# Two attention layers with experts on one core: the first layer's normals move to GpSimd, and twelve of eighteen weight products move from the first layer's end to the second layer's start

## What is computed

```
x = x + xattn0(layernorm(x), ctx)            # 16 heads of 16
x = x + experts(layernorm(x))                # 8 experts, one per token, 512 places each, else x
x = x + xattn1(layernorm(x), ctx)            # 16 heads, biases, then relu(.@W1+b1)@W2+b2
x = x + cell(layernorm(x))                   # 6 nodes of attention, 8 heads of 32, then a layernorm
# one node c of the cell; src, edge: fixed small tables
q = ew[c,0]*(nodes[src_q] @ We[eq] + be[eq]) ; k, v likewise with ew[c,1], ew[c,2]
nodes[c] = act_w[c]*mha(q,k,v; Wq[c],Wk[c],Wv[c],Wo[c]) + q
```

## Time and profile before

| | us |
|---|---|
| median of 3 runs | 4257.91 (4254.85 to 4258.33) |
| the profiled execution | 4261.87 |
| its span, first to last instruction | 4260.1 |
| PE busy | 4052.2 (95%) |
| ACT busy | 2647.2 (62%) |
| DVE busy | 2515.5 (59%) |
| POOL busy | 1774.9 (42%) |
| mean granted clock of PE, share of 2.4 GHz | 0.978 |

### The profile page before, as it was taken

The page is one execution under the profiler, slowest core; times in us unless marked ns, Lnnn a source line. Parts: engine busy times, 40 slices in busy tenths (PEclk is TensorE's granted clock), DMA queues, the critical chain, the costliest instruction groups (busy, mean ns, idle before and its releaser), DMA issues.

```text
span 4260.1 us, 100693 instructions
## 1 busy us (share of the span) xinstructions
PE 4052.2 (95%) x38276; PEld 3431.3 (81%) x38276; DVE 2515.5 (59%) x6280; ACT 2647.2 (62%) x11818; POOL 1774.9 (42%) x1883
## 2 busy tenths in 40 slices
...
DMA packets 117867, 129.75 MB, mean 30 GB/s; under 512 B 12006, under 2 KB 110676, under 8 KB 117264
## 3 DMA queue, kind: packets, MB, share of 16 engines
...
## 4 chain that ended last, share of the span: by engine, by line
PE 58%; DVE 9%; ACT 5%; POOL 3%; issue 1%; DMA 0%; SPq 0%; POOLq 0%; DVEq 0%
PE c_product L1297 26%; PE c_product L1308 12%; PE c_product L1348 8%; PE c_scores L1338 6%; ACT c_front_probs L1118 4%; PE c_product L1371 4%; DVE c_neg_max L1173 2%; DVE c_xn L1158 2%; DVE c_routed L1158 1%; PE c_product L1359 1%; DVE c_x L1183 1%; POOL c_rstd L1064 1%; ACT c_probs L1118 1%; POOL c_probs L1076 1%; PE c_product L1285 1%
## 5 line engine op out<-in xcount | busy, mean ns | idle before, releaser
L1118 ACT ACTIVATE c_probs<-c_scores,c_neg_max 128x128 f32<-128x128 f32 x3072 | 1081.9, 407 | 480.5 <-DVE c_neg_max L1173 480.5
L1076 POOL TENSOR_TENSOR c_probs<-c_probs,c_row_inv 128x512 f32<-128x512 f32 x768 | 790.5, 1041 | 1211.3 <-DVE c_row_inv L1176 1208.7
L1297 PE MATMUL c_product<-c_nodes,cell_w 128*128 128x256 f32 x4352 | 1056.9, 383 | 2.7 <-DVE c_nodes L1164 1.0
L1297 PEld LDWEIGHTS c_product<-c_nodes,cell_w 128*128 128x128 f32 x4352 | 803.5, 190 | 124.8 <-issue 19.6
L1173 DVE TENSOR_REDUCE c_neg_max<-c_scores 128x4 f32<-128x512 f32 x1024 | 635.7, 683 | 254.9 <-PE c_scores L1338 254.9
L1118 ACT ACTIVATION_READ_ACCUMULATOR c_probs<-c_scores,c_neg_max 128x1 f32 x3072 | 757.7, 247 | 0.0
L1124 ACT COPY c_probsT<-c_product 128x512 f32<-128x512 f32 x768 | 413.3, 613 | 440.4 <-PE c_product L1348 440.4
L1308 PE MATMUL c_product<-cell_w,c_nodes 128*128 128x256 f32 x1792 | 435.4, 383 | 0.0
L1118 ACT ACTIVATE c_front_probs<-c_scores,c_neg_max 128x128 f32<-128x128 f32 x1024 | 358.3, 403 | 116.7 <-DVE c_neg_max L1173 116.7
L1348 PE MATMUL c_product<-consts_sb,c_probs 128*128 128x128 f32 x3072 | 398.8, 276 | 14.8 <-POOL c_probs L1076 13.7
L1348 PEld LDWEIGHTS c_product<-consts_sb,c_probs 128*128 128x128 f32 x3072 | 350.9, 142 | 47.8 <-POOL c_probs L1076 19.8
...
## 6 DMA issues: line engine op xcount, KB each, us to landing
...
a_x<-in_x SPq DMA_DIRECT2D x32, 256.0 KB, 3.4
a_ctxT<-in_ctx_pairsT SPq DMA_DIRECT2D x32, 256.0 KB, 3.5
x<-a_x SPq DMA_DIRECT2D x32, 256.0 KB, 2.1
xn<-a_xn SPq DMA_DIRECT2D x32, 256.0 KB, 2.2
c_routed<-xn SPq DMA_DIRECT2D x32, 256.0 KB, 2.9
c_x<-x SPq DMA_DIRECT2D x32, 256.0 KB, 3.0
c_ctxT<-in_ctx_pairsT SPq DMA_DIRECT2D x32, 256.0 KB, 2.7
```

The costliest lines, as they stand in the source:

```text
L1076: nc.gpsimd.tensor_tensor(e, e, rinv[:, i, r].unsqueeze(2).broadcast_to([P, 4, T]), ALU.mult).then_inc(norm_made, 1)
L1118: a = nc.scalar.activation(probs(n)[:, r, k], S[r][:, k], ACT.Exp, bias=nmax[:, i, r, k:k + 1], accum_out=rsum[:, i, r, k:k + 1])
L1297: i = T_.matmul(m[:, u], w[:, k, u * P:(u + 1) * P], src[:, k], start=n == 0, stop=n == last)
```

## The change

1. First layer: `nm` and `nm1` (four instructions a job, 128x256 with two operations each) go from DVE to POOL, with buffers of statistics doubled; DVE's `bn_aggr` gets a wait for the normal two jobs back. `K^O` goes from ACT to DVE, behind `K^`. `w.s` is taken out. `xn1` has 6 places instead of 8. All four order tables are new, with longer lags (`r.n:4` becomes `r.n:6`).
2. F0 to F5 and B0 to B5 stay at the first layer's end, the other twelve pairs go to the second layer's first steps. Their inputs go through a ring of four that lies in the buffers of the cell's probabilities, unused until then. Loads of number 6 to 9 are started by ACT, those from 10 on by SP.
3. Experts: SP loads the plain weights for node e-1 behind the loads of expert e, POOL scales them. DVE turns the first rows out (`rows_turned(0)`) before it waits for `b2`, not after.
4. Second layer: the rows, the context and three weights are loaded first, by SP; the other weights by ACT, each with a semaphore of its own. Before, SP started all twelve ahead of the rows. The four order tables are new.

The core of the diff (of the tables, the lines that the prediction speaks of):

```diff
 FIRST_POOL_ORDER = """
-S0.n1:1 S0.n2:1 S0.n3:1 S1.n0:1 S1.n1:1 S1.n2:1 w.s:6 rs1:2 S1.n3:1 put:9 rs:-1 S0.n0:0
+rs:1 nm:1 rs1:4 S0.n0:2 nm1:4 S0.n1:2 S1.n0:2 S1.n1:2 S1.n3:2 S1.n2:2 S0.n3:2 S0.n2:2 put:9
 """
 FUSE_PE_PLACES = """
-...
-r.n:0 F8 F9 B8 B9 F10 F11 B10 B11 F12 F13 B12 B13 F14 F15 B14 B15 F16 F17 B16 B17
+Tn:1 F0
+L:1 B0
+Tn:0 F1
+L:0 B1 F2 F3
+r.n:0 B2 B3 F4 F5 B4 B5
 """
+            def normal(src, dst, i, j, made):
+                pool.wait_ge(rstd_made[i], j + 1)
+                for b in range(PAIR):
+                    k = nc.gpsimd.tensor_scalar(dst[:, b], src[:, b], mv[:, i, j % 2, b, 0:1], rstd[:, i, j % 2, b:b + 1],
+                                                ALU.subtract, ALU.mult)
+                k.then_inc(made, 1)
...
+                elif n == "nm":
+                    if j >= 1:
+                        pool.wait_ge(prod, n_prod["Tx", j - 1])
+                    normal(xt[:, j % X_RING], xn, 0, j, xn_made)
...
+                    V.tensor_scalar(kE[:, o], m, cst[:, C_EVEN:C_EVEN + 1], None, ALU.mult)
+                    V.tensor_scalar(kO[:, o], m, cst[:, C_ODD:C_ODD + 1], None, ALU.mult).then_inc(prod_used, 1)
...
+            rows_turned(0)
             dve.wait_ge(b2_in, 16)
-            rows_turned(0)
...
 PE_ORDER = """
-V1:1 K2:1 Q4:2 T1.0:1 f.Tb0.1:0 S4:2 T1.1:1 K5:2 V4:2 A1:1 f.Ab0:0 O1:1 T4.0:2 T4.1:2 f.Sb1:0 A4:2 Q2:1 O4:2
+f.Tb0.1:0 V1:1 O3:2 K2:1 T1.0:1 Q4:2 T1.1:1 S4:2 f.V:0 K5:2 V4:2 A1:1 T4.0:2 f.Sb1:0 O1:1 f.Ab0:0 T4.1:2 Q2:1
+f.Tb1.0:0 A4:2 S2:1 f.Tb1.1:0 O4:2 f.Ab1:0 Q5:2 f.W1a:0 f.W1b:0 T2.0:1 S5:2 f.W2:0 K3:1 V2:1 T2.1:1 V5:2
+LATE_FUSE_PE_PLACES = """
+start:0 F6 B6 F7 B7 F8 B8 F9 B9 F10
+f.Tx:0 B10
+f.Q:0 F11
+f.Sb0:0 B11 F12 F13 B12 B13 F14
+f.Tb0.0:0 B14
+f.Ab0:0 F15 F16 B15
+f.Tb1.0:0 B16 F17
+f.Tb1.1:0 B17
+"""
...
+            load_rows(0)
+            load_context(0)
+            for t, a, got in ((wk, "L1_xattn_Wk_rows", wk_in), (wq, "L1_xattn_Wq", wq_in), (wv, "L1_xattn_Wv_rows", wv_in)):
+                sp.dma_start(t[:], halves(io[a])).then_inc(got, 16)
+            fuse_load(FUSED_FIRST + LATE_RING)
+            load_rows(1)
+            for n in range(FUSED_FIRST + LATE_RING + 1, len(fused)):
+                fuse_load(n)
+            load_context(1)
```

More of the change, by code:

```diff
@@ L64, in cell_plan, with fused_weights @@
     return plan
+def fused_weights(plan):
+    return [(c, k, plan[c]["edge"][k]) for c in range(NODES) for k in (TO_Q, TO_K, TO_V)]
 def unfold(table, jobs):
@@ L71, in unfold, with with_fused @@
     return [(name, k - s) for k in range(min(first, 0), jobs + last) for name, s in order if 0 <= k - s < jobs]
+def with_fused(order, table, job_of, at):
+    order = list(order)
+    for line in table.strip().splitlines():
+        behind, *pieces = line.split()
+        name, k = behind.split(":")
+        i = 0 if name == "start" else order.index((name, job_of(int(k)))) + 1
+        order[i:i] = [(p, at) for p in pieces]
+    return order
 def counted(order, test):
@@ L138, in phase_first_layer @@
     W2 = PAIR * T
[L139 removed]
+    X_RING, ROW_RING, GROUP = 4, 6, 4
     MASK_JOBS, SENDS, RING = 4, 3, 3
     plan = cell_plan()
[L142 removed]
+    fused = fused_weights(plan)
     SCALE = 1.0 / np.sqrt(D // CELL_HEADS)
[L144 removed]
     PAIRS_OF_HEADS = D // 32
@@ L868 @@
 PE_ORDER = """
-f.Tx:0 T0.1:1 S3:2 f.K:0 f.Q:0 K4:2 K1:1 A0:1 f.Sb0:0 T3.0:2 O0:1 f.V:0 T3.1:2 Q1:1 f.Tb0.0:0 A3:2 S1:1 O3:2
-V1:1 K2:1 Q4:2 T1.0:1 f.Tb0.1:0 S4:2 T1.1:1 K5:2 V4:2 A1:1 f.Ab0:0 O1:1 T4.0:2 T4.1:2 f.Sb1:0 A4:2 Q2:1 O4:2
-f.Tb1.0:0 f.Tb1.1:0 S2:1 V5:2 f.Ab1:0 Q5:2 f.W1a:0 f.W1b:0 S5:2 f.W2:0 K3:1 T2.0:1 V2:1 f.Txn:0 T5.0:2 T2.1:1
-K0:0 T5.1:2 Q0:0 A2:1 A5:2 S0:0 V0:0 O2:1 O5:2 T0.0:0 Q3:1 V3:1
+S3:2 T0.1:1 f.Tx:0 f.K:0 V3:2 f.Q:0 A0:1 f.Sb0:0 K1:1 O0:1 T3.0:2 K4:2 T3.1:2 Q1:1 A3:2 f.Tb0.0:0 S1:1
@@ L884 @@
+f.Sb1.x3:0 f.Sb1.i0:0 O1^:1 f.Sb1.i1:0 f.Ab0^:0 f.Sb1.i2:0 f.Sb1.i3:0 Q2^:1 A4^:2 S2.x0:1 S2.x1:1 S2.x2:1
+S2.x3:1 S2.i0:1 O4^:2 S2.i1:1 f.Ab1^:0 S2.i2:1 Q5^:2 S2.i3:1 f.W1a^:0 f.W1b^:0 S5.x0:2 S5.x1:2 S5.x2:2 S5.x3:2
+S5.i0:2 f.W2^:0 S5.i1:2 f.st3:0 S5.i2:2 K3^:1 S5.i3:2 f.nm3:0 f.Txn^:0 A2^:1 Q0^:0 A5^:2 K0^:0 O2^:1 S0.x0:0
+S0.x1:0 S0.x2:0 S0.x3:0 S0.i0:0 O5^:2 S0.i1:0 e.st:2 S0.i2:0 Q3^:1 S0.i3:0 e.nm:2
 """
 ACT_ORDER = """
-V3^:2 T0^2:1 T0^3:1 S3.e0:2 S3.e1:2 S3.e2:2 S3.e3:2 T3^0:2 T3^1:2 f.Sb0.e0:0 f.Sb0.e1:0 f.Sb0.e2:0 f.Sb0.e3:0
@@ new lines @@
+f.Sb1.n2:0 f.Sb1.n3:0 S2.n0:1 S2.n1:1 S2.n2:1 S2.n3:1 S5.n0:2 S5.n1:2 f.rs3:0 S5.n2:2 S5.n3:2 f.x3b:0 S0.n0:0
+S0.n1:0 e.rs:2 S0.n2:0
+"""
+LATE_FUSE_PE_PLACES = """
[8 more added lines that the diff above has]
+"""
+LATE_FUSE_DVE_PLACES = """
+start:0 F6^ B6^ F7^
+f.x2:0 B7^
+f.st:0 F8^ B8^
+f.x:0 F9^ B9^ F10^
+f.Tx^:0 B10^
+f.Q^:0 F11^
+f.x2:1 B11^
+f.Sb0.i1:0 F12^
+f.Sb0.i3:0 B12^ F13^ B13^
@@ L909, in phase_second_layer @@
+f.x:1 F14^ B14^
+f.Sb1.i0:0 F15^
+f.Ab0^:0 F16^
+f.Sb1.i2:0 B15^
+f.Sb1.i3:0 B16^ F17^ B17^
+"""
+def phase_second_layer(nc, io, scratch, keep, cell, cst, out):
     ctx = io["ctx_pairsT"]
@@ L1046, in _, with fuse_load @@
                 sp.dma_start(ct[:], halves(ctx[j])).then_inc(c_in[j % 2], 16)
+            def fuse_load(n):
+                sp.wait_ge(prod, n_prod[f"B{n - LATE_RING}", 0])
+                late_load(sp, n)
+            load_rows(0)
[7 more added lines that the diff above has]
+            load_context(1)
+            for j in range(2, JOBS):
+                load_rows(j)
+                load_context(j)
                 if j >= JOBS_IN_FLIGHT:
```

255 lines of the change are left out of this document (133 added, 122 removed).

## The result

The changed kernel takes 4162.27 us (median of 4 runs, 4160.97 to 4164.93), the kernel before 4257.22 beside it (4254.85 to 4258.33): ratio 0.9772, 95% interval 0.9759 to 0.9784, 95 us less. 4161 was forecast. The profiled execution's span fell from 4260.1 to 4159.2 us, by 100.9.

A forecast was written before the change was run, and what follows sets the result against it. POOL waiting for DVE's reciprocals was taken to hold up PE in the first layer, PE itself to bind the second; terms -42 + 3 - 36 - 6 + 4 - 20 = -97 gave 4161 us at the median, range 4118 to 4210.

The forecast's parts named there:

- first layer's 30 steps: First layer's loop: 17.7 us a step plus routing groups and misfits, 550 us instead of 592, -42.
- its end: First layer's end: fewer F and B pieces, phase ending about 19 us behind the last normal, -36 (-25 to -45).
- experts: Experts' start: DVE copies the turned rows at about 724.8 instead of 730.56, -6 us; scaling costs nothing.
- second layer's head: Second layer's start: moved F and B pieces mostly hidden in waits, clock gives some back, together +4 us.
- its loop: Second layer's loop: two PE waits go, 1.3 us a job, new short covers cost 0.5; -20 us taken.
- the forecast's circle with PE: First layer: POOL's serial list in a step plus 5.8 us of PE's part closes a loop of 17.5 us.
- The price: First layer: one normal on POOL was taken to cost 1.0 us, with bounds 0.63 and 1.84.
- The routing groups: First layer's loop: some seven groups of routing work, 1.5 us each, against some 8 us before.
- 9 us added for misfits: First layer's loop: allowance for small misfits of a hand-made order, raising 541 us to 550.
- rival of a POOL-bound layer: First layer: at 1.5 us a normal the step is 19.5, loop 595 instead of 550, 4206 us; chance 0.13.
- `r.oh` at the head of DVE's step: First layer's routing groups: placed there, only `K^` and `Tx^` behind it come late, 1.5 us a group.
- the new short covers: Second layer's loop: three places with one 0.9 us piece between product and copy's user, costing 0.5 us a job.

The follow-up runs named there:

- e2: Changed kernel with the first layer's normals on POOL doing only the subtraction, one operation instead of two: 4180.56 us, ratio 0.9794.
- e3: Changed kernel with two more normals on POOL in each first-layer step: 4258.66 us in one execution.
- e8: Changed kernel with the second layer's head loads earlier and `nm1` later in POOL's first-layer list: 4186.98 us, ratio 0.9808.
- e4: Changed kernel with both first-layer normals, `nm` and `nm1`, back on DVE: 4223.25 us, ratio 0.9892.
- e6: Changed kernel with `K^` and `st` ahead of the routing pieces in DVE's first-layer list: 4158.57 us, ratio 0.9763.
- e7: Changed kernel with the twelve F and B pieces at the first layer's end in another order: 4162.46 us, ratio 0.977.
- e1: Kernel before with only the changed kernel's four second-layer order tables, run twice: 4259.53 and 4261.27 us, ratio 0.9978 both times.
- e9: Changed kernel with the old second-layer order tables, all twelve late F and B pieces at the head: 4225.08 us, ratio 0.9903.

## Why the prediction was right

**Overall.** The time was 1 us off, and partly by luck: the terms were off by up to 9 us, in both directions.

| term | forecast | measured |
|---|---|---|
| start | +3 | +0.8 |
| first layer's 30 steps | -42 | -34.7 |
| its end | -36 | -27.2 |
| experts | -6 | -5.7 |
| second layer's head | +4 | -1.2 |
| its loop | -20 | -27.1 |
| behind the last `f.Txn` | 0 | -5.8 |
| sum | -97 | -100.9 |

**What bounds the loop of the first layer.** Right as a mechanism: POOL's list sets the undisturbed step (e2, e3), and in after the forecast's circle with PE closes, with waits of 0.2 to 0.3 us at both joints. But the list alone is as long within 0.1 us (e8), so a shorter circle gains nothing, which the forecast didn't say. The price was mis-sized, 1.23 us and not 1.0, the step not, 17.81 for 17.7: my circle of 17.5 at 1.0 us would be 18.4 at 1.23, so its other parts were 0.6 too long. The routing groups cost 2.9 to 4.2 us and not 1.5, some 23 us in all; with 9 us added for misfits the sum had 19. For `w.s` the text has 18.8 us and the sum no term of its own; in its six steps the loop gained 25.4, and only 10.7 in the 19 steps behind them. How much of the 34.7 the move of the normals gives is not shown (e4). The rival of a POOL-bound layer is half true: it binds, and costs 10 us (e2), not 45. That `r.oh` at the head of DVE's step leaves only small delays failed: A waited 1.8 us for `K^`'s bank, and e6 showed that another place is no cheaper.

The Trainium skill's GPSIMD Engine Reference, section "Key points", has GpSimd contend with VectorE's instructions that use both its ports or have two SBUF inputs. If the normals did, the divisions on POOL should have become a little faster when they left VectorE. The rows don't show it, 1040 ns before and 1047 after; in which mode the normals ran no row tells.

**The first layer's end.** The term that failed most, -27 for -36. "Twelve puts behind the last `nm1`, 15.4, and 3.4 to land": the puts were not one row, the last four waited 6.0 us for `slots`, since the last routing chain ran later than I had put it; and from the last put's start to the next phase took 7.9 us where 3.4 were allowed. The landing took only 2.1 of them; the rest is POOL's DRAIN, 5.29 us, and some 0.5 us around it, a term that the sum didn't have, since before it was hidden under the F and B. That puts and not PE set the end was right (e7). The Trainium skill, Perfetto Trace Analysis, section "DMA Instruction — SWDGE (GPSIMD)", says that such an instruction's end in the profile is the last descriptor's writing and not the data's movement. The trace agrees: the last put's own record ends 1.0 us behind its start, and its landing is seen at 2.1.

**Experts.** -5.7 for -6. PE waits 0.8 us for the copy that no longer stands behind `b2`, and 7.1 before; no run moved the copy alone. The plain weights' scaling beside PE's work cost nothing seen: PE is busy without a gap from 700 to 890 us.

**Second layer's head.** `f.Tx` +1.2 (forecast +1), F11's wait 2.4 (1.5), `f.Tb0.0` +3.7 behind `f.Tx` (3.5): the pieces up to there right. From `f.Tb0.0` to `f.Txn(0)` it took 29.6 us instead of 35.8, -6.1, where I had +3 for pieces and -5 for the clock. With pieces in it the stretch got shorter. The granted clock in it was 0.67 before and 0.99 after. PE is busy 25.1 and 24.8 us there, but after has three F and four B more in it, some 9.7 us; so, as an estimate, the same other work took 15 us instead of 25, and the clock gave back some 10 us of PE's time where I had allowed 5. e1 and e9, which have no pieces in this stretch, took 35.5 and 34.9 us, and every kernel with the pieces there 29.6 to 30.1. e9 prices the places: 26 us.

**Second layer's loop.** The two waits of the earlier trace rows went, 1.28 us a job, and 0.97 was gained; so the new short covers cost 0.3 us and not 0.5, and none of them long enough for the profile to list it as a wait. The waits go with the order alone and come back with the old one (e1, e9); the loop's full gain by the order alone was not measured, since e1 ran only on chips with the hold. -27 for -20. What comes behind the last `f.Txn` I had left out of the sum: 5.8 us, also the order's (e1, e9).
